# Five opening ticks of a two-stage expert kernel written out one by one, and the second weight matrix loaded behind the first gather

## The chip, the cores and the metric

The kernel runs on one core of a Trainium2 chip. The metric is the device time of one execution in microseconds; times given for the kernel before are 254.93, 255.06 and 255.61 us (median 255.06).

The core's engines run in parallel, each through its own queue in program order, and wait for each other through semaphores: TensorE (PE: matrix products and transposes), VectorE (DVE), ScalarE (ACT), GpSimd (POOL, which also issues the indirect DMAs: gathers and scatters) and SyncE (SP, which issues the plain loads).

## What is computed

Two layers of routed experts on 2048 tokens of width 512:

```python
x = x + _L0_xattn_ref(_layernorm(x, axis=-1), itok_BxS_13_99985, ctx_2048, ctx_2048, ctx_2048)
x = x + _L0_ffn_ref(_layernorm(x, axis=-1), L0_ffn_router_w, L0_ffn_wg, L0_ffn_wu, L0_ffn_wd)
```

The first layer picks one of four experts by the token's id. An expert has one matrix C (512 x 512, the context), used three times:

```python
expert_ids = jnp.minimum(tid // tokens_per_expert, E - 1)
g = jax.nn.silu(jnp.einsum('bsd,fd->bsf', hidden_states, Wg[e]))
u = jnp.einsum('bsd,fd->bsf', hidden_states, Wu[e])
y = jnp.einsum('bsf,df->bsd', g * u, Wd[e])
```

As Wg and Wu are the same matrix, one product a = h C^T serves both. The second layer picks one of eight experts by the largest of eight logits, and its weights are made ternary:

```python
s = 1.0 / jnp.clip(jnp.mean(jnp.abs(w)), EPS, None)
return jnp.clip(jnp.round(w * s), -1.0, 1.0) / s
```

24 weight matrices (1 MB each in 32 bit) have to be loaded, their mean absolute value taken, scaled, rounded and cut. The activations are rounded to eight bits by row.

## The kernel before

Tokens are sorted by expert into blocks of 128 rows: 19 blocks for the first layer (`B1`), 23 for the second (`B2`). The sorting takes the first 10 us. Then a pipeline runs over blocks b. For the first layer, block b passes through:

- POOL `gather(b)` (L465): an indirect DMA brings the block's rows from memory into `x`
- DVE `moments_of`, `aggregate`, `normalise`, `variance`: mean and variance, and `h` = x minus its mean
- PE `transpose_h`; ACT `evict_hT` (L758) writes the transposed rows as the high half `hT_hi`; DVE `hT_rest` (L1083) writes what that leaves out as `hT_lo`
- PE `first_product` (L1585) through `product1` (L1542): three passes of four matmuls of 512 columns, high by high, high by low, low by high halves, with the context's halves `ctx_hi` and `ctx_lo`
- ACT `silu` (L740), DVE `gate` (L1090): p = silu(a) a
- PE `transpose_p`; ACT `evict_pT`, DVE `pT_rest` (L1097); PE `second_product` (L1612): again three passes
- DVE `residual` (L1106) and `negative_mean`: the new row; ACT `square`, DVE `largest` and several small POOL operations (`quantising`): what the second layer's rounding needs
- PE `transpose_x1`, ACT `evict_x1T`, PE `logits`, DVE `top_logits` (L1132), `choice`, `one_hot`, PE `rank` and `count_in`, DVE `row_index`, POOL `place` and `store`: the route of the second layer and a scatter of the rows to scratch memory

`high_halves(e)` (ACT for e = 0 and 1, POOL for 2 and 3) and DVE `low_half(e, part)` (L994) split the context of expert e.

Beside it the weight matrices are made ternary, one a tick: `load_weights(i)` on SP (L364), `sum_abs(i)` on ACT (L680), `sum_mean(i)` on PE (L1566), `mean_of(i)` and `scale_of(i)` on DVE, `scale_part(i)` on both ACT (three quarters) and DVE (one quarter), `cut(i)` on DVE. The matrices 0, 1, 4, 5, ... go through two staging tiles, so `load_weights(4)` waits for both `scale_part(0)`, and `load_weights(5)` for both `scale_part(1)`; 2 and 3 have places of their own. All loads stand in one queue, SP's.

The order on each engine is written by hand. A tick t of the loops (`for t in range(2, TICKS)` on ACT, L843, and DVE, L1392; `for t in range(2, B1)` on PE, L1803) holds first_product(t), second_product(t - 1) and the logits of t - 2; what comes before tick 2 is written out. Before transpose_h(0), PE runs nine matmuls on constants (`warm_up`, L1782), and three behind it. A product on PE waits for its operands before its first pass (`hT_hi` and `ctx_hi` for the first two blocks, `hT_lo` for the others). Of the inputs' 18 blocks in use, block 0 belongs to expert 0, block 1 to expert 1, blocks 2 and 3 to expert 2, and the others to expert 3.

The loads at the start stand on SP in this order:

```python
            load_context(0)
            load_weights(0)
            load_context(1)
            load_weights(1)

            sp.wait_ge(gathering, 2)
            load_context(2)
            load_weights(2)
            load_weights(3)
            load_context(3)
```

`gathering` counts the gathers that POOL has handed out.

## Time and profile before

| | |
|---|---|
| times | 254.93, 255.06, 255.61 us |
| profiled execution | 255.76 us |
| its span | 253.8 us |
| PE busy | 234.7 us (92%) |
| PE weight loads (beside the matmuls) | 172.4 us (68%) |
| DVE busy | 218.2 us (86%) |
| ACT busy | 210.5 us (83%) |
| POOL busy | 164.2 us (65%) |
| loads by SP's queue | 37.91 MB, 42.4% of the DMA engines' time |

The profile is one execution; its times in the rows below are microseconds from the start of its span. A row of the timeline gives start, duration, engine, source line, operation, output and inputs, and in brackets how long the engine idled before it and what ended that. Matmuls overlap, so the distance from one start to the next tells more of their cost than the duration.

### The profile page before, as it was taken

How to read it: one execution, taken by the hardware profiler on the slowest of the kernel's cores; microseconds unless marked ns; L12 is line 12 of the kernel's file. 1: busy time of each engine (PE TensorE's matmuls, PEld its weight loads, DVE VectorE, ACT ScalarE, POOL GpSimd, SP SyncE). 2: the span in 40 equal slices, each digit the busy share in tenths (PEclk: the TensorE clock that was granted, in tenths of full speed). 3: DMA queues.
4: the chain of work that ended last, by engine and by line, in shares of the span. 5: the costliest groups of instructions: out<-in, count | busy, mean ns of one | idle time of the engine just before them, and what ended most of it. 6: DMA issues, size and time to landing. Idle time of an engine off the chain costs nothing.

```text
span 253.8 us, 5722 instructions
## 1 busy us (share of the span) xinstructions
PE 234.7 (92%) x1409; PEld 172.4 (68%) x1419; DVE 218.2 (86%) x675; ACT 210.5 (83%) x324; POOL 164.2 (65%) x325
## 2 busy tenths in 40 slices
PE   2398999999999999999999999999999999999990
PEld 2255778888888888888888888886455555555530
DVE  5879989899889988799888988879999999999871
ACT  2767899799888988898888888787899999999960
POOL 4362665868778777588777664347538786757653
PEclk9999999999999999999999999999999999999996
DMA  5999944935754499784566534541388962211110
GB/s 203 425 359 362 424 180 151 362 131 226 243 210 146 134 354 406 283 324 157 201 249 227 147 127 169 207 146 69 98 237 250 310 251 85 83 41 68 70 37 0
DMA packets 13726, 51.71 MB, mean 204 GB/s; under 512 B 2750, under 2 KB 2750, under 8 KB 10112
## 3 DMA queue, kind: packets, MB, share of 16 engines
q1 hardware_dynamic: 8816, 37.91, 42.4%
q0 software_dynamic: 4880, 13.44, 14.4%
q8 instruction: 14, 0.23, 0.3%
q14 instruction: 16, 0.13, 0.1%
HBM read 40.49 MB, written 13.48 MB: 213 GB/s over the span
## 4 chain that ended last, share of the span: by engine, by line
PE 73%; DVE 10%; DMA 9%; issue 4%; ACT 1%; POOL 1%; SPq 0%; DVEq 0%; ACTq 0%
PE bank L1555 33%; PE bank L1677 19%; PE bank L1539 9%; PE bank L1647 5%; DMA staged<-weight_chunks 4%; PE bank L1669 4%; DMA ternary<-weight_chunks 3%; PE bank L1784 2%; DMA staged<-x_rows 1%; DVE ternary L957 1%; DVE ctx_lo L1000 1%; PE bank L1574 1%; POOL out_rows L643 1%; DVE ternary L1019 1%; DMA token_ids<-token_ids_in 1%
## 5 line engine op out<-in xcount | busy, mean ns | idle before, releaser
L1677 PE MATMUL bank<-ternary,qT 128*128 x179 | 43.6, 380 | 0.5
L694 ACT ACTIVATE ternary<-staged 128x2048 bf16<-128x2048 f32 x20 | 38.0, 1899 | 2.5 <-DMA staged<-weight_chunks 2.5
L700 ACT ACTIVATE ternary<-staged,w_scale 128x1536 int16<-128x1536 f32 x20 | 31.4, 1576 | 2.3 <-DVE w_scale L1014 0.6
L1677 PEld LDWEIGHTS bank<-ternary,qT 128*128 128x128 bf16 x184 | 17.7, 97 | 20.2 <-issue 5.4
L562 POOL DMA_INDIRECT x_rows<-row,store_at x19 | 25.5, 1340 | 6.8 <-POOL store_at L554 5.0
L643 POOL DMA_INDIRECT out_rows<-late_rows,late_token x18 | 19.0, 1057 | 9.4 <-DVE late_rows L1350 8.0
L473 POOL DMA_INDIRECT x<-x_rows,gather x16 | 18.5, 1155 | 10.2 <-DVE gather L969 6.3
L1677 PE MATMUL bank<-ternary,rT 128*128 x87 | 22.6, 380 | 0.4 <-ACT rT L812 0.2
L747 ACT ACTIVATE p<-bank,rstd 128x512 f32<-128x512 f32 x19 | 13.0, 684 | 11.6 <-PE bank L1555 11.5
L1555 PE MATMUL bank<-ctx_hi,pT_hi 128*128 x76 | 22.3, 415 | 0.1
L1555 PE MATMUL bank<-ctx_hi,hT_hi 128*128 x76 | 22.3, 414 | 0.0
L1094 DVE SCALAR_TENSOR_TENSOR p<-bank,rstd,p 128x512 f32<-128x512 f32 x19 | 14.2, 749 | 9.3 <-ACT p L747 9.3
L1647 PEld LDWEIGHTS bank<-router,x1T 128*128 128x128 f32 x152 | 19.7, 191 | 1.9 <-ACT x1T L756 0.6
L1555 PE MATMUL bank<-ctx_lo,hT_hi 128*128 x76 | 20.4, 391 | 0.3 <-DVE ctx_lo L1000 0.3
L1555 PE MATMUL bank<-ctx_lo,pT_hi 128*128 x76 | 20.5, 392 | 0.0
L1555 PE MATMUL bank<-ctx_hi,pT_lo 128*128 x76 | 20.5, 392 | 0.0
L1555 PE MATMUL bank<-ctx_hi,hT_lo 128*128 x76 | 20.3, 389 | 0.0
L517 POOL TENSOR_TENSOR row<-ln,half_powers 128x2 f32<-128x2 f32 x19 | 14.5, 763 | 8.8 <-DVE squares L1129 8.7
L1647 PE MATMUL bank<-router,x1T 128*128 128x8 f32 x152 | 18.2, 247 | 0.1
L489 POOL TENSOR_TENSOR rstd<-var_eps,half_powers 128x1 f32<-128x1 f32 x19 | 13.7, 719 | 5.3 <-DVE var_eps L1070 4.8
L1305 DVE TENSOR_TENSOR prod<-bank,relu 128x512 f32<-128x512 f32 x23 | 15.8, 686 | 1.5 <-ACT relu L790 0.6
L1555 PEld LDWEIGHTS bank<-ctx_lo,hT_hi 128*128 128x128 f32 x76 | 14.2, 188 | 3.6 <-issue 0.7
(237 smaller groups left out, 658.6 us busy)
## 6 DMA issues: line engine op xcount, KB each, us to landing
staged<-weight_chunks SPq DMA_DIRECT2D x20, 1024.0 KB, 5.5
late_rows<-x_rows SPq DMA_DIRECT2D x18, 260.0 KB, 3.7
ternary<-ctx_chunks SPq DMA_DIRECT2D x4, 1024.0 KB, 8.3
ternary<-weight_chunks SPq DMA_DIRECT2D x4, 1024.0 KB, 9.8
x_rows<-filler SPq DMA_DIRECT2D x1, 2080.0 KB, 12.9
staged<-x_rows SPq DMA_DIRECT2D x5, 260.0 KB, 2.7
x_rows<-row,store_at POOLq DMA_INDIRECT x19, 6.0
out_rows<-late_rows,late_token POOLq DMA_INDIRECT x18
```

Of the source, the lines that this page charges most:

```text
L473: pool.indirect_dma_start(x[b % RING], None, x_in, bass.IndirectOffsetOnAxis(ap=gather1[:, b:b + 1], axis=0), bounds_check=last_token, oob ...
L517: pool.tensor_tensor(r[:, RSTD:INV + 1], s[:, 2:4], half_powers[:, :], ALU.pow).then_inc(norm2, 1)
L562: pool.indirect_dma_start(x1_rows, bass.IndirectOffsetOnAxis(ap=store_at[b % ROWS][:, :], axis=0), row[b % ROWS][:, :], None, bounds_check ...
L643: pool.indirect_dma_start(out, bass.IndirectOffsetOnAxis(ap=token, axis=0), cols_of([b], 0, D), None, bounds_check=last_token, oob_is_err= ...
L694: nc.scalar.activation(ternary[:, m * K * D:(m + 1) * K * D], staged_of(i), ACT.Abs, accum_out=abs_sum[:, 2 * i:2 * i + 1]).then_inc(abs_r ...
L700: nc.scalar.activation(ternary[:, m * K * D + DVE_COLS:(m + 1) * K * D].bitcast(I16), staged_of(i)[:, DVE_COLS:], ACT.Copy, scale=w_scale[ ...
L1094: dve.scalar_tensor_tensor(p[:, :], a_ps[b % 2][:, :], rstd1[b % 2][:, :], p[:, :], ALU.mult, ALU.mult).then_inc(p_ready, 1)
L1305: dve.tensor_tensor(prod[b % 2][:, :], u_ps[b % 2][:, :], relu2[:, :], ALU.mult)\
L1539: last = pe.transpose(ps[:, k * P:(k + 1) * P], src[:, k * P:(k + 1) * P], ident[:, :])
L1555: last = pe.matmul(ps[:, :], left[:, k * P:(k + 1) * P], right[:, bass.ds(e * (K * D) + k * D, D)], start=(n == 0 and k == 0), stop=(n == ...
L1647: last = pe.matmul(logits_ps[:, 0:E2], x1T[:, k * P:(k + 1) * P], router[:, k * E2:(k + 1) * E2], start=(k == 0), stop=(k == K - 1))
L1677: last = pe.matmul(ps[:, :], left[:, k * P:(k + 1) * P], ternary[:, bass.ds(e * (3 * K * D) + (kind * K + k) * D, D)], start=(k == 0), sto ...
```

## The change

On SP, the second weight matrix is issued once the first gather is handed out; context 2 and weights 2 follow once the second gather is, weights 3 once context 2 has landed, and context 3 once weights 2 has. On ACT, DVE and PE, ticks 2 to 4 are written out operation by operation in a new order, and the loops begin at tick 5 (`OPENING`). Seven matmuls stand ahead of transpose_h(0) in place of nine. `product1` can run other work of PE ahead of its second or third pass (`ahead`), and the products of blocks 1 to 3 wait for less at their start: the first product for `hT_hi` and the high halves of the context, the second product of block 0 for `pT_hi`. The work done is the same.

```diff
-WARM_UP = (9, 3)
+WARM_UP = (7, 3)
+OPENING = 5
...
             load_context(1)
+            sp.wait_ge(gathering, 1)
             load_weights(1)
-
             sp.wait_ge(gathering, 2)
+
             load_context(2)
             load_weights(2)
+            sp.wait_ge(ctx_in_sem[2], 16)
             load_weights(3)
+            sp.wait_ge(staged_early_in[0], 16)
             load_context(3)
```

ScalarE:

```diff
             high_halves(1)
-            sum_abs(1)
             evict_hT(0)
             scale_part(0)
+            sum_abs(1)
+            evict_hT(1)
+            silu(0)
+            sum_abs(2)
+            evict_pT(0)
             scale_part(1)
-            silu(0)
-            evict_hT(1)
-            evict_pT(0)
-            sum_abs(2)
             silu(1)
             evict_hT(2)
+            sum_abs(3)
             scale_part(2)
-            sum_abs(3)
-            for t in range(2, TICKS):
+            evict_pT(1)
+            evict_x1T(0)
+            square(0)
+            silu(2)
+            sum_abs(4)
+            evict_hT(3)
+            evict_pT(2)
+            scale_part(3)
+            scale_part(4)
+            sum_abs(5)
+            silu(3)
+            square(1)
+            evict_hT(4)
+            evict_x1T(1)
+            scale_part(5)
+            evict_pT(3)
+            sum_abs(6)
...
+            for t in range(OPENING, TICKS):
```

VectorE, the added order of the first ticks (the removed one is in the listing above):

```diff
+            low_half(0, 0)
             mean_of(0)
-            scale_of(0)
-            low_half(0, 0)
             moments_of(0)
             aggregate(0)
             normalise(0)
-            variance(0)
             low_half(0, 1)
-            mean_of(1)
-            scale_of(1)
-            hT_rest(0)
-            low_half(1, 0)
+            scale_of(0)
             moments_of(1)
             aggregate(1)
             normalise(1)
+            hT_rest(0)
+            variance(0)
             variance(1)
-            scale_part(0)
-            gate(0)
-            hT_rest(1)
+            low_half(1, 0)
             low_half(1, 1)
...
             moments_of(2)
             aggregate(2)
             normalise(2)
+            gate(0)
+            hT_rest(1)
+            mean_of(1)
+            scale_of(1)
+            low_half(2, 0)
             variance(2)
+            scale_part(0)
+            pT_rest(0)
+            low_half(2, 1)
             mean_of(2)
             scale_of(2)
+            gate(1)
             moments_of(3)
             aggregate(3)
+            residual(0)
+            negative_mean(0)
+            hT_rest(2)
+            normalise(3)
             variance(3)
+            scale_part(1)
+            moments_of(4)
+            mean_of(3)
+            scale_of(3)
+            aggregate(4)
+            pT_rest(1)
+            gate(2)
+            low_half(3, 0)
+            low_half(3, 1)
+            mean_of(4)
+            scale_part(2)
+            scale_of(4)
+            residual(1)
+            negative_mean(1)
+            hT_rest(3)
+            scale_part(3)
+            scale_part(4)
+            top_logits(0)
+            choice(0)
+            one_hot(0)
+            pT_rest(2)
+            normalise(4)
+            largest(0)
+            moments_of(5)
+            variance(4)
+            mean_of(5)
+            gate(3)
+            scale_of(5)
+            row_index(0)
+            aggregate(5)
+            variance(5)
+            cut(4)
+            residual(2)
+            negative_mean(2)
+            scale_part(5)
+            hT_rest(4)
+            largest(1)
+            top_logits(1)
+            choice(1)
+            one_hot(1)
+            normalise(5)
+            pT_rest(3)
+            largest(2)
+            gate(4)
...
+            cut(5)
```

TensorE, the waits and the new order:

```diff
-            def first_product(b):
+            def first_product(b, ahead={}):
...
-                if b < 2:
+                if b < E1:
                     pe.wait_ge(hT_hi_ready, b + 1)
-                    pe.wait_ge(ctx_hi_ready, b + 1)
+                    pe.wait_ge(*((ctx_hi_ready, b + 1) if b < 2 else (pool_hi_ready, b - 1)))
                     pe.wait_ge(centred, 1)
                 else:
                     pe.wait_ge(hT_lo_ready, b + 1)
...
             transpose_h(0)
-            sum_mean(1)
             warm_up(WARM_UP[1])
             first_product(0)
             load_expert(1)
             transpose_h(1)
-            transpose_p(0)
-            first_product(1)
+            sum_mean(1)
+
+            def in_first1():
+                transpose_p(0)
+            first_product(1, {2: in_first1})
             load_expert(2)
             transpose_h(2)
-            sum_mean(2)
-            second_product(0)
-            for t in range(2, B1):
+
+            def in_second0():
+                sum_mean(2)
+            second_product(0, {1: in_second0})
+
+            def in_first2():
+                transpose_p(1)
+                transpose_x1(0)
+                sum_mean(3)
+            first_product(2, {2: in_first2})
+            load_expert(3)
+            transpose_h(3)
+            second_product(1)
+            transpose_p(2)
+            sum_mean(4)
+
+            def in_first3():
+                logits(0)
+            first_product(3, {2: in_first3})
+            load_expert(4)
+            transpose_x1(1)
+
+            def in_second2():
+                rank(0)
+                sum_mean(5)
+                transpose_h(4)
+            second_product(2, {2: in_second2})
+            transpose_p(3)
+
+            def in_first4():
+                logits(1)
+            first_product(4, {2: in_first4})
+            load_expert(5)
+            count_in(0)
+            transpose_x1(2)
+            transpose_h(5)
+            rank(1)
+            sum_mean(6)
+            second_product(3)
+            logits(2)
+            count_in(1)
+            for t in range(OPENING, B1):
```

## Rows read from the trace of the kernel before

**Rows 1.** Page, the chain that ended last: shares of the span by engine.

```profile
PE 73%; DVE 10%; DMA 9%; issue 4%; ACT 1%; POOL 1%; SPq 0%; DVEq 0%; ACTq 0%
```

**Rows 2.** Stretches: start:end, length, busy PE, PEld, DVE, ACT, POOL, PEclk, DMA share, GB/s.

```profile
12.69:16.51 3.82, 3.82 (x10) 1.38 (x11) 2.93 (x7) 2.81 (x3) 2.10 (x4) 1.00 0.98 360
16.51:30.57 14.06, 12.62 (x61) 9.27 (x59) 13.18 (x25) 10.09 (x11) 6.93 (x6) 1.00 1.01 386
...
55.60:63.59 7.99, 7.99 (x51) 6.82 (x51) 7.45 (x25) 7.63 (x12) 7.00 (x12) 1.00 0.54 203
```

**Rows 3.** Timeline (start, us, engine, line), TensorE: opening to the first second_product.

```profile
12.69 4.02 PE L1784 MATMUL bank<-iota 128*128 128x512 f16 x9 [0.29 <-issue]
...
16.51 1.06 PE L1539 MATMUL bank<-ident,h 128*128 128x128 f32 x4
...
17.56 0.81 PE L1784 MATMUL bank<-iota 128*128 128x512 f16 x3
...
18.34 1.17 PE L1555 MATMUL bank<-ctx_hi,hT_hi 128*128 x4
...
27.73 1.17 PE L1555 MATMUL bank<-ctx_hi,pT_hi 128*128 x4
```

**Rows 4.** Timeline, TensorE: tick 3 from first_product to tick 5.

```profile
39.62 1.17 PE L1555 MATMUL bank<-ctx_hi,hT_hi 128*128 x4
...
42.48 0.63 PE L1539 MATMUL bank<-ident,row 128*128 128x128 f32 x4
...
43.68 1.19 PE L1555 MATMUL bank<-ctx_hi,pT_hi 128*128 x4
...
46.54 0.95 PE L1647 MATMUL bank<-router,x1T 128*128 128x8 f32 x8
...
47.37 0.64 PE L1539 MATMUL bank<-ident,p 128*128 128x128 f32 x4
...
47.76 1.17 PE L1555 MATMUL bank<-ctx_hi,hT_hi 128*128 x4
...
55.60 0.64 PE L1539 MATMUL bank<-ident,p 128*128 128x128 f32 x4
```

**Rows 5.** Timeline, VectorE: moments and h of block 0.

```profile
14.80 0.69 DVE L1058 BATCH_NORM_STATS2 stats<-x 128x6 f32<-128x512 f32 x1 [0.81 <-DMA x<-x_rows,gather]
...
15.74 0.49 DVE L1080 TENSOR_SCALAR h<-x,moments 128x512 f32<-128x512 f32 x1
```

**Rows 6.** Timeline, VectorE, ticks 3 and 4.

```profile
40.12 0.68 DVE L1114 SCALAR_TENSOR_TENSOR row<-bank,x 128x512 f32<-128x512 f32 x1
...
40.73 0.17 DVE L1136 MAX8 best<-bank 128x8 f32<-128x8 f32 x1
...
41.41 0.48 DVE L1080 TENSOR_SCALAR h<-ternary,moments 128x512 f32<-128x512 f32 x1
...
44.21 0.75 DVE L1094 SCALAR_TENSOR_TENSOR p<-bank,rstd,p 128x512 f32<-128x512 f32 x1
...
45.74 0.68 DVE L1087 TENSOR_TENSOR hT_lo<-bank,hT_hi 128x512 fp32r<-128x512 f32 x1
...
47.36 0.69 DVE L1025 TENSOR_SCALAR ternary<-ternary 128x2048 bf16<-128x2048 int16 x1
```

**Rows 7.** Timeline, ScalarE: an evict_hT, sum_abs(2), a silu.

```profile
17.60 0.60 ACT L764 ACTIVATE hT_hi<-bank 128x512 fp32r<-128x512 f32 x1 [1.52 <-PE bank L1539]
...
24.79 1.91 ACT L694 ACTIVATE ternary<-ternary 128x2048 bf16<-128x2048 f32 x1 [0.60 <-DMA ternary<-weight_chunks]
...
43.46 0.68 ACT L747 ACTIVATE p<-bank,rstd 128x512 f32<-128x512 f32 x1
```

**Rows 8.** DMA issues in 11.7:12.5 us (gather 1); last figure: us, issue to landing.

```profile
x<-x_rows,gather POOLq DMA_INDIRECT x1, 3.6
```

**Rows 9.** DMA issues in 13:13.3 us (gather 2).

```profile
x<-x_rows,gather POOLq DMA_INDIRECT x1, 9.7
```

**Rows 10.** DMA issues in 40:41 us (a load alone in its queue).

```profile
staged<-weight_chunks SPq DMA_DIRECT2D x1, 1024.0 KB, 4.8
```

72 lines of the change are left out of this document (36 added, 36 removed).

## The prediction

> **What bounds the kernel now.** I read the chain that ended last first [rows 1]: 73% of it is TensorE (PE), so time is to be had only where PE waits. Then the stretches [rows 2]: from 55.60 us a tick of 7.99 us has 7.99 us of PE work, and it stays so for the rest of the first product stage. The opening, 16.51 to 30.57, has 12.62 busy of 14.06 us, at a DMA share of 1.01 and with VectorE (DVE) busy for 13.18. So the change can win only what PE idles before 55.60, which is where tick 5 begins, with the same work done in both kernels: from there both run the same loop. My whole sum is one number: when transpose_p(4) starts in the new kernel, against 55.60 [rows 4].
>
> Short names: F, S are first_product and second_product, Th, Tp, Tx the three transposes, each with its block. PE work, from the distance of one start to the next [rows 4]: F 2.83 (39.62 to about 42.45), S 2.86, logits 0.81, Tp 0.39; Th and Tx about 0.45 (an estimate between Tp and the 0.6 that one lasts); sum_mean, rank and count_in together 0.2 a tick. A product's last result is 0.16 later than the next start. Handing on between engines costs 0.03 to 0.13. DVE, start to start [rows 5, 6]: gather landed to h 1.43 (14.80 to 15.74 + 0.49), low_half 1.13 (an estimate: about 1.8 times the 0.61 of residual, for twice the columns), gate 0.67, hT_rest 0.61 with its result at 0.68, residual 0.8 with its accumulator and negative_mean, top_logits to one_hot 0.68, scale_part 0.4, cut 0.61. ScalarE (ACT) [rows 7]: sum_abs 1.9, evict_hT 0.60, silu 0.68; scale_part lies between, about 1.5.
>
> **The change part by part.** *Start.* Nine warm-ups take 12.69 to 16.51, 0.425 each [rows 3]; seven end at 15.66. h(0) is wanted by then. Gather 0 is issued at about 10.3, and its data were waited for until 14.80 [rows 5]; gather 1 took 3.6 us [rows 8]. With weights 1 out of the way I take 3.6 for gather 0 too, so 13.9, and h(0) at 15.35: transpose_h(0) starts at 15.66, a gain of 0.85. Between the ends 3.6 and 4.5 I take the lower, because the queue is then empty behind context 1. Part of the gain goes back at once: the nine warm-ups run at 512 columns in 0.425 us, the level of 1.2 GHz, the later three in 0.81 together [rows 3], which is 2.4 GHz (the clock column says 1.00 for both, so it can't be used here). PE rose between 16.51 and 17.56, with the engine busy since 12.69. If it rises at the same moment, the three late warm-ups start 1.05 us earlier and run partly at the low level: F0 starts at 17.48 to 17.8; I take 17.65 against 18.34, as the middle.
>
> *F0 to S0.* F0 ends at 20.5; Th(1); ACT evicts it by 21.8, after sum_abs(1). That sum now stands behind scale_part(0), which ends at 18.7; weights 1, issued at about 11.75 and not at 3, lands at 16.6 to 18 (4.8 us alone in its queue [rows 10], plus gathers), so its cover is 0.7 us and the cost is nothing. F1 starts at 21.9, with 0.8 us of idle PE. ctx_lo(1) is now ready at 21.1, since both its halves stand before moments_of(2), so nothing waits inside F1; Tp(0) goes in before its third pass, and Th(2) ends PE's work at 25.7. S0 needs evict_pT(0), which stands behind sum_abs(2) on ACT: everything on ACT waits for weights 2 there. Before, weights 2 was there at 24.79 [rows 7]. Now it shares the queue with weights 1 and context 2 alone (weights 3 is issued once context 2 is in, context 3 once weights 2 is): three loads of 1.05 MB and about 0.55 MB of gathers are 3.7 MB, from 13.5 on (issue, and the part of the 4.8 us that isn't transfer) at the 360 to 386 GB/s of [rows 2] 9.6 to 10.3 us, so 23.1 to 23.8, or 22.3 if the gathers are through early; I take 22.9. Then 1.9 + 0.6 + handing on: S0 starts at 25.7, against 27.73 [rows 3]. That is the change's whole gain, 2.0 us. Each us that weights 2 lands after 23.0 costs 1.0; at 24.7, as before, 1.65.
>
> *S0 to F3.* Work: 2.86 + 0.14, then 2.83 + 0.39 + 0.45 + 0.14 (F2 with Tp(1), Tx(0) and a mean inside), 0.45, 2.86, 0.39 + 0.14 = 10.65, plus 0.15 of wait for pT_rest(1): F3 at 36.5. F3 to S2: 2.83 + logits(0) 0.81 + Tx(1) 0.45 = 4.1, but pT_rest(2) follows top_logits, choice and one_hot of block 0, which need logits(0): 0.15 more. S2 at 40.85. Weights 3 and 4 have 2 us and more of cover here: weights 4 is issued at 25.7, late by 4 us since scale_part(0) on DVE moved back, and wanted at 33.5. On the POOL queue gather 3 now stands behind the inverse deviation of block 0, 2 us later, wanted at 28.2. largest(0) comes much later too, so quantising(0) on POOL ends only just before residual(2) needs it; what that could cost is in the upper end.
>
> *S2 to F4, where the gain is lost.* F4 waits for hT_rest(4) (block 4 takes the branch of b >= E1). On DVE that stands behind residual(2), negative_mean(2) and scale_part(5), and residual(2) needs the end of S2. Chain from S2's start: two passes, a rank and sum_mean(5) 2.25; mean_of(5) was waiting for that; then gate(3) 0.67, cut(4) 0.61 and five small ones about 0.6 (three dependent ones take 0.68 [rows 6]): 4.15. S2 itself is ready at 3.6, so DVE is the later. Then 0.8 + 0.4 + 0.68 + 0.05: F4 starts 6.1 after S2, at 46.95. PE has 2.86 + 0.17 + 0.45 + 0.39 = 3.87 of work in it: 2.2 us idle. Had DVE come in time, it would still be 0.16 + 0.8 + 0.4 + 0.68 + 0.05 - 0.39 = 1.7. Before, F4 started at once behind Tp(3), 0.39 after 47.37 [rows 4].
>
> *F4 to tick 5.* 2.83 + 0.81 + 0.45 + 0.45 + 0.2 + 2.86 + 0.81 = 8.4, nothing waits: the chain from logits(1) over one_hot, normalise(5) and pT_rest(3) takes 1.8, PE's way to S3 2.0, so that is covered by only 0.2. Tick 5 at 55.4.
>
> The sum: 25.7 + 10.8 + 4.35 + 6.1 + 8.45 = 55.4 against 55.60, 0.2 us less. The profiled execution took 255.76 us (span 253.8), the median of the three runs is 255.06, 0.7 less; so 255.56 for such an execution, and **254.9 us** for the median.
>
> **The rivals.** A measurement of this kernel can tell about 0.3%, 0.77 us, from no change.
>
> *A, the forecast:* 2.0 us won by S0, given back ahead of F4. 254.9, own range 254.3 to 255.8. Chance 0.45.
>
> *B, faster:* DVE reaches residual(2) before S2 ends (idle 1.7 and not 2.2), the two small waits of 0.15 are not there, and F0 starts at 17.48: 0.95 less, 254.0. For it speaks that hand-offs are summed on the slow side; against it that the stall's 1.7 is fixed by the order of the program. Chance 0.28.
>
> *C, slower: gather 2 isn't there when it is wanted.* moments_of(2) now comes at 20.85, ahead of gate(0) and no longer behind it; gate(0) stands behind it, and Tp(0) and all of PE behind gate(0). Gather 2 took 9.7 us from 13.1 [rows 9], so 22.8. With up to 0.75 of slack, it costs one for one from 21.6 on: 1.2 at 22.8, so 256.1; slower than before by over 0.3% from 22.5 on. For it: the DMA share is about 1 in both, and issue is no earlier. Against: gathers 1 [rows 8] and 0 took 3.6 and 4.5 while at most two loads stood ahead, 9.7 was with four issued behind it. The Trainium skill, "DMA: Bandwidth & Descriptors" (Arbitration), says that an engine takes turns between its queues packet by packet; by that rule two loads in the queue or four make no difference to a gather, and the time would be the 256.1 of this case. The rows lean against the rule (3.6 and 9.7 at the same share), though not by an experiment. Chance 0.17.
>
> *D, slower: the clock.* PE idles 2.2 us before F4. The opening of before has 1.44 us of idle PE in all (14.06 less 12.62 [rows 2]), and no single gap of 2.2. At the low level F4's twelve matmuls take 5.1 us (0.425 each [rows 3]) and not 2.83: 257.2. The Trainium skill, "TensorE: Matmul & The Clock Gate" (The HAM clock gate), has the array fall back after idling; the trace can't show whether this gap is enough. Chance 0.05.
>
> *E, it doesn't do what it says:* gather 0 lands at 14.78 as before, h(0) at 16.25, 0.6 lost: 255.5. Chance 0.05.
>
> **How the numbers follow.** Faster is B, 0.28; within 0.3% is A and E, 0.50; slower is C and D, 0.22. Range: down to B with 0.4 for the hand-offs, 253.6; up past C to the case that weights 2 lands at 24.7 (254.9 + 1.65 = 256.55), 256.7. D is left out.
>
> **What would show it.** transpose_h(0) at 15.7, F0 at 17.6, F1 at 21.9, S0 at 25.7 or a wait of ACT for weights 2 ahead of it; F3 about 3 us before 39.62 (2.3 of it real, since logits(0) is inside it now); a 2 us hole of PE ahead of the product of block 4, released by DVE's hT_lo; transpose_p(4) at 55.4, then ticks of 7.99. The forecast is wrong if that hole is not there, if the opening loses to a landing (moments_of(2) idle for a gather, sum_abs(2) for weights), or if the twelve matmuls of block 4 last 5 us.

## The result, and the profile after

The changed kernel takes 261.45 us (median; 261.4 to 262.84), against 255.34 us (254.93 to 255.88) for the kernel before on the same chip: a ratio of 1.025, 95% interval 1.021 to 1.029. It is slower by 2.5%, where 254.9 us was forecast. The profiled execution took 261.4 us, its span 259.4. It can be set beside the 255.76 us and 253.8 of the kernel before: 5.6 more.

The forecast was one walk to the start of transpose_p(4), tick 5. The TensorE rows of the timeline after (start, us, engine, line, operation; in brackets the idle time before it and what ended that) go through the same points:

```profile
15.64 1.06 PE L1613 MATMUL bank<-ident,h 128*128 128x128 f32 x4
...
17.47 1.51 PE L1632 MATMUL bank<-ctx_hi,hT_hi 128*128 x4
...
21.34 1.19 PE L1632 MATMUL bank<-ctx_hi,hT_lo 128*128 x4 [1.46 <-DVE hT_lo L1116]
...
23.74 1.19 PE L1632 MATMUL bank<-ctx_hi,hT_hi 128*128 x4 [0.65 <-ACT hT_hi L772]
24.77 1.09 PE L1632 MATMUL bank<-ctx_lo,hT_hi 128*128 x4
28.08 0.97 PE L1613 MATMUL bank<-ident,p 128*128 128x128 f32 x4 [2.21 <-DVE p L1123]
28.70 2.06 PE L1632 MATMUL bank<-ctx_hi,hT_lo 128*128 x4
30.55 1.06 PE L1613 MATMUL bank<-ident,h 128*128 128x128 f32 x4
31.26 1.36 PE L1632 MATMUL bank<-ctx_hi,pT_hi 128*128 x4
...
42.11 1.17 PE L1632 MATMUL bank<-ctx_hi,hT_hi 128*128 x4
...
46.47 1.20 PE L1632 MATMUL bank<-ctx_hi,pT_hi 128*128 x4
...
52.72 1.19 PE L1632 MATMUL bank<-ctx_hi,hT_hi 128*128 x4 [2.03 <-DVE hT_lo L1116]
...
61.36 0.64 PE L1613 MATMUL bank<-ident,p 128*128 128x128 f32 x4
```

| point or stretch | forecast | after | before [rows 3, 4] |
|---|---|---|---|
| transpose_h(0) | 15.66 | 15.64 | 16.51 |
| F0 | 17.65 | 17.47 | 18.34 |
| F1 | 21.9 | 23.74 | |
| S0 | 25.7 | 31.26 | 27.73 |
| S0 to F3 | 10.8 | 10.85 | |
| F3 to S2 | 4.35 | 4.36 | |
| S2 to F4, with the hole | 6.1 | 6.25 | |
| F4 to tick 5 | 8.45 | 8.64 | |
| tick 5 | 55.4 | 61.36 | 55.60 |

Tick 5 is 5.76 us later than before, and that is the whole 5.6: from there the tick takes 7.99 us again, with PE busy throughout, as in [rows 2]. S0 came 5.56 us later than walked, although F0 began 0.18 early: the miss lies between these two points. The four stretches behind S0 came within 0.2 us each, 0.4 together. Three things happened ahead of S0.

*Gather 1 was late.* VectorE stood 2.58 us for it (first row below is gather 0, which came as forecast), and hT_rest(0), put behind normalise(1) by the new order, stood behind that. F0's third pass waited 1.46 us for it, and F1 started at 23.74.

```profile
14.04 0.69 DVE L1087 BATCH_NORM_STATS2 stats<-x 128x6 f32<-128x512 f32 x1 [0.83 <-DMA x<-x_rows,gather]
...
19.25 0.69 DVE L1087 BATCH_NORM_STATS2 stats<-x 128x6 f32<-128x512 f32 x1 [2.58 <-DMA x<-x_rows,gather]
```

The DMA issues of 11.7:11.9 us after (first fence: the last figure is us from issue to landing) give gather 1 7.4 us, where [rows 8] had 3.6. The shares of the two queues in 13.8:14.2 us of the kernel before (second fence) and in 14.6:15.2 of the one after (third) tell why. In the kernel before, weights 1 had just been through and context 2 had not begun, so GpSimd's queue (software) had the engines to itself. In the kernel after, weights 1 was flowing on SyncE's queue (hardware), and between 14.0 and 15.5 us no packet of a gather moved, though two gathers were handed out at 11.79 and 13.10. From 16.5 to 19.5 us, beside context 2, they had 27.7% of the engines' time.

```profile
x<-x_rows,gather POOLq DMA_INDIRECT x1, 7.4
```

```profile
q0 software_dynamic: 42, 0.14, 97.7%
```

```profile
q1 hardware_dynamic: 32, 0.26, 104.2%
```

*normalise(2) took 2.83 us in place of 0.49.* In the new order it stands ahead of gate(0), on which transpose_p(0) and all of PE wait. It ended at 27.36, which is 0.29 us after GpSimd's cast of context 2 ended (25.17 + 1.90 = 27.07). VectorE and GpSimd after:

```profile
24.53 2.83 DVE L1109 TENSOR_SCALAR h<-x,moments 128x512 f32<-128x512 f32 x1
27.29 0.74 DVE L1123 SCALAR_TENSOR_TENSOR p<-bank,rstd,p 128x512 f32<-128x512 f32 x1
```

```profile
25.17 1.90 POOL L489 CAST ctx_hi<-ternary 128x2048 fp32r<-128x2048 f32 x1
```

*TensorE's clock fell in the hole.* PE stood 2.21 us ahead of transpose_p(0). The windows after (us; busy us and count for PE, PE's weight loads, VectorE, ScalarE, GpSimd; granted clock, DMA share, GB/s) show a granted clock of 0.57 and 0.58 behind it, so for most of these 4 us the lower level, 1.2 GHz in place of 2.4:

```profile
26.00:28.00 2.00, 0.00 (x0) 0.00 (x0) 2.00 (x3) 0.07 (x1) 1.82 (x2) 1.00 0.93 360
28.00:30.00 2.00, 1.92 (x7) 1.70 (x8) 1.97 (x7) 0.91 (x2) 0.31 (x1) 0.57 0.88 326
30.00:32.00 2.00, 2.00 (x8) 1.63 (x8) 2.00 (x5) 2.00 (x3) 0.67 (x1) 0.58 0.71 158
```

F1's third pass was 1.85 us ahead of the next start, transpose_h(2) 0.71. Without the fall the same two take 1.05 and 0.35 (e4 below: 27.72, 28.77, 29.12). That is 1.16 us by S0, and 0.18 more in S0's first pass.

Together: 1.84 (F1 late) + 2.21 (hole) + 1.16 (clock) + 0.23 (from transpose_p(0) to F1's third pass, 0.62 and not 0.39) = 5.44 of the 5.56. The 0.23 is a wait that the walk had left out: the third pass needs hT_lo(1), and hT_rest(1) stands behind gate(0) on VectorE, where it took 27.95 to 28.63; the pass began at 28.70.

### The profile page after: what moved, and what is told of

It reads as the page before. It is cut to its first block, busy times and chain, and to the rows that moved or that the text cites. A ratio compares the mean times of both kernels' runs of the same rounds, so it can differ in the third digit from the quotient of the medians.

```text
span 259.4 us, 5720 instructions
## 1 busy us (share of the span) xinstructions
PE 235.9 (91%) x1407; PEld 173.8 (67%) x1417; DVE 219.5 (85%) x675; ACT 210.0 (81%) x324; POOL 162.8 (63%) x325
## 4 chain that ended last, share of the span: by engine, by line
PE 80%; DVE 10%; DMA 4%; issue 3%; POOL 1%; SPq 0%; DVEq 0%
PE bank L1632 40%; PE bank L1759 19%; PE bank L1613 10%; PE bank L1729 6%; PE bank L1751 4%; DMA x<-x_rows,gather 3%; DVE h L1109 1%; DMA staged<-x_rows 1%; PE bank L1651 1%; DVE ternary L986 1%; DVE ctx_lo L1029 1%; POOL out_rows L651 1%; DMA token_ids<-token_ids_in 1%; DVE late_rows L1379 1%; DVE p L1123 1%
## 5 line engine op out<-in xcount | busy, mean ns | idle before, releaser
L570 POOL DMA_INDIRECT x_rows<-row,store_at x19 | 24.5, 1292 | 6.8 <-POOL store_at L562 5.9
L1123 DVE SCALAR_TENSOR_TENSOR p<-bank,rstd,p 128x512 f32<-128x512 f32 x19 | 14.2, 749 | 10.5 <-ACT p L755 10.3
L1632 PE MATMUL bank<-ctx_hi,hT_lo 128*128 x76 | 21.7, 410 | 1.5 <-DVE hT_lo L1116 1.5
L497 POOL TENSOR_TENSOR rstd<-var_eps,half_powers 128x1 f32<-128x1 f32 x19 | 14.1, 741 | 12.4 <-DVE var_eps L1099 11.9
L1632 PEld LDWEIGHTS bank<-ctx_hi,hT_lo 128*128 128x128 f32 x76 | 14.4, 195 | 4.6 <-DVE hT_lo L1116 1.9
## 6 DMA issues: line engine op xcount, KB each, us to landing
x_rows<-filler SPq DMA_DIRECT2D x1, 2080.0 KB, 12.6
```

The lines of the kernel that those rows point to most:

```text
L570: pool.indirect_dma_start(x1_rows, bass.IndirectOffsetOnAxis(ap=store_at[b % ROWS][:, :], axis=0), row[b % ROWS][:, :], None, bounds_check ...
L1123: dve.scalar_tensor_tensor(p[:, :], a_ps[b % 2][:, :], rstd1[b % 2][:, :], p[:, :], ALU.mult, ALU.mult).then_inc(p_ready, 1)
L1632: last = pe.matmul(ps[:, :], left[:, k * P:(k + 1) * P], right[:, bass.ds(e * (K * D) + k * D, D)], start=(n == 0 and k == 0), stop=(n == ...
```

## The experiments

Every ratio is against the kernel before, run on the same chip, with its 95% interval in brackets. 0.003 is about what can be told from 1. F, S, Th, Tp are the names of the prediction. A time in brackets after a start is the idle time before it.

### Loads and order apart: e1_loads_only, e2_order_only

e1 is the kernel before with the new loads; e2 is the changed kernel with the old ones. The edit of e2 (that of e1 is the same lines the other way round):

```diff
             load_context(1)
-
-            sp.wait_ge(gathering, 1)
             load_weights(1)
+
             sp.wait_ge(gathering, 2)
-
             load_context(2)
             load_weights(2)
-            sp.wait_ge(ctx_in_sem[2], 16)
             load_weights(3)
-            sp.wait_ge(staged_early_in[0], 16)
             load_context(3)
```

> The kernel before, with the new order of loads alone. Theory (gather 1 was slowed by weights 1, which now starts beside it): gather 1 takes about 7 us and not 3.6, but costs nothing here, because VectorE comes to moments_of(1) only at about 20; weights 1 lands at 16.6 and sum_abs(1) stands ahead of evict_hT(0) on ScalarE, so first_product(0) starts at 19.3 and not 18.34, and the kernel takes 1.1 us more, 256.4. Rival (the loads have nothing to do with it): gather 1 takes 3.6 to 4.5 us and the time stays at 255.3. Second rival (the loads are all of the loss): 261.

> The changed kernel with the loads in the order of before. Theory: gather 1 takes 3.6 to 4.5 us again and the 2.6 us idle of VectorE before moments_of(1) is gone; gather 2 takes 9.7 us again and lands at 22.8, weights 2 at 24.7, so second_product(0) starts at about 27.4, the 2.2 us hole ahead of the product of block 4 stays: 256.9. Rival (the new order loses by itself, whatever the loads do): 261.

Measured: e1 1.010 [1.006, 1.013], e2 1.017 [1.011, 1.023]. Each half costs by itself, and both expectations were too good (1.1 us over 255.3, or 1.004, and 256.9, or 1.006). The rival of e2, that the new order loses by itself (261, or 1.022), lies inside its interval. In e1, weights 1 comes later, and in the old order ScalarE's sum_abs(1) stands ahead of evict_hT(0), and sum_mean(1) ahead of PE's three warm-ups. PE stood 2.12 us, and F0 began at the lower clock. TensorE of e1:

```profile
18.96 0.38 PE L1578 MATMUL bank<-abs_sum,ones 128*128 128x1 f32 x2 [2.12 <-ACT ternary L698]
...
20.01 2.27 PE L1559 MATMUL bank<-ctx_hi,hT_hi 128*128 x4
```

In e2, with weights 1 issued at once, gather 1 took 4.2 us, VectorE did not wait for it, and F1 started at 21.97, where 21.9 had been walked. The 1.46 us wait of F0 is gone. The collision with the cast (normalise(2) 2.45 us) and the fall of the clock stayed. VectorE, then TensorE of e2:

```profile
22.97 2.45 DVE L1105 TENSOR_SCALAR h<-x,moments 128x512 f32<-128x512 f32 x1
```

```profile
26.14 0.66 PE L1609 MATMUL bank<-ident,p 128*128 128x128 f32 x4 [2.06 <-DVE p L1119]
26.74 2.07 PE L1628 MATMUL bank<-ctx_hi,hT_lo 128*128 x4
```

So the late gather comes from the loads, the collision from the order. e2 also speaks against my reading that a gather is slow by the number of loads issued behind it: gather 2 took 8.9 us in e2 with all loads issued and 8.2 in the changed kernel with two.

### One cause at a time in the changed kernel: e3_cast_held, e4_filled, e5_weights1_last, e6_rest4_early

e3 holds GpSimd's cast of context 2 until normalise(2) is through:

```diff
                 pool.wait_ge(ctx_in_sem[e], 16)
+                if e == 2:
+                    pool.wait_ge(h_ready, 3)
                 pool.tensor_copy(
```

> The changed kernel, where GpSimd's cast of context 2 (high_halves(2)) waits for h(2). Theory (VectorE's normalise(2) lasted 2.83 us because it was shut out until GpSimd's cast had ended, and PE's clock fell in the hole that this made): normalise(2) lasts 0.5 to 1 us, transpose_p(0) starts at 25.8 and not 28.08, the matmuls behind it run at the high level: 3.7 us less, 257.7. Rival (the 2.83 us have another cause, as the inverse deviation or the gather's descriptors): normalise(2) stays near 2.8 us and the time at 261.4. If only the lock is right and not the clock: 259.1.

Measured: 1.027 [1.022, 1.032], no gain at all, though what was meant to happen did: normalise(2) 0.49 us, Tp(0) at 25.94, S0 at 27.93, 3.3 us earlier than after. VectorE and GpSimd of e3:

```profile
24.74 0.49 DVE L1111 TENSOR_SCALAR h<-x,moments 128x512 f32<-128x512 f32 x1
...
36.54 0.69 DVE L1089 BATCH_NORM_STATS2 stats<-ternary 128x6 f32<-128x512 f32 x1 [1.64 <-DMA ternary<-x_rows,gather]
```

```profile
25.61 1.89 POOL L491 CAST ctx_hi<-ternary 128x2048 fp32r<-128x2048 f32 x1
27.68 2.02 POOL L481 DMA_INDIRECT ternary<-x_rows,gather  x1 [0.18 <-issue]
```

The gain went to the next thing that was late. The new order has moments_of(4) ahead of pT_rest(1). Gather 4, which stands behind the cast on GpSimd, was issued at 27.68 (27.25 after), and its data ended VectorE's wait at 36.54, 8.9 us later (5.1 us of transfer after). S1 stood 2.45 us for pT_rest(1), and F4 2.03 us as before. The profiled execution of e3 took 265.84 us, 2.65 over its median, with a mean granted clock of 0.972; behind the 2.45 us its rows show the lower level too (S1's first pass 1.87 us from start to start), and again inside F4, so in this execution part of what was won went there.

e4 gives PE eight matmuls on constants ahead of Tp(0), so that the hole is there for everyone but the clock:

```diff
             def in_first1():
+                warm_up(8)
                 transpose_p(0)
```

> The changed kernel with eight matmuls on constants put into the hole of PE ahead of transpose_p(0), 1.7 of its 2.2 us. Theory (PE's clock fell because it idled there): the granted clock stays 1.00 between 28 and 32 us, transpose_p(0) starts at 28.1 as before, and the 1.4 us that the low level took are saved: 260.0. Rival (the clock fell for another reason, or its fall costs nothing, since other engines are late there too): 261.4 or more.

Measured: 1.020 [1.012, 1.027], 259.97 us, about as expected (260.0, a ratio of 1.018). normalise(2) was still 2.83 us and ended 0.28 after the cast, PE stood only 0.48 us, and the clock stayed:

```profile
27.12 0.66 PE L1613 MATMUL bank<-ident,p 128*128 128x128 f32 x4 [0.48 <-DVE p L1123]
27.72 1.21 PE L1632 MATMUL bank<-ctx_hi,hT_lo 128*128 x4
```

The pass that took 2.06 us after takes 1.21, and from Tp(0) to S0 e4 takes 2.00 us, the changed kernel 3.18. The ratios differ by 0.6%, 1.4 us, but their intervals overlap ([1.012, 1.027] and [1.021, 1.029]), and gather 1 took 6.5 us here, so that F1 started 0.95 us earlier. So what the filling is worth in the whole time isn't shown; what the clock costs is read from the rows. One of e4's four executions took 262.82 us with a mean granted clock of 0.978 (the others 0.994 to 0.996), so filling this one hole doesn't keep the clock up every time.

e5 issues weights 1 behind gathering 2, so that nothing flows beside gather 1; e6 puts hT_rest(4) ahead of cut(4) and residual(2):

```diff
-            sp.wait_ge(gathering, 1)
-            load_weights(1)
             sp.wait_ge(gathering, 2)
+            load_weights(1)
 
             load_context(2)
```

```diff
+            hT_rest(4)
             cut(4)
             residual(2)
             negative_mean(2)
             scale_part(5)
-            hT_rest(4)
```

> The changed kernel with weights 1 issued behind the second gather and not behind the first. Theory (a gather is slow when a large load flows beside it, and how many stand in the queue matters little): gather 1 takes 4 to 5 us and not 7.4, the 2.6 us of VectorE before moments_of(1) and the 1.5 us inside first_product(0) go, second_product(0) starts 1.5 us or more earlier than 31.3 at the same hole ahead of transpose_p(0): 259.5. Rival (gather 1 is slow because gather 0 goes before it, or by its own rows): gather 1 stays at 7 us, the time at 261.4.

> The changed kernel with hT_rest(4) on VectorE moved ahead of cut(4), residual(2), negative_mean(2) and scale_part(5). Theory (first_product(4) waits only for that position): its wait shrinks from 2.0 us to 0.3 or less and the time falls by 1.7 to 2.0: 259.5. Rival (what is late there is ScalarE's evict_hT(4), or the loss comes back a step later because residual(2) is now late): 261.4, with a new wait of second_product(3).

Measured: e5 1.011 [1.008, 1.014], e6 1.011 [1.007, 1.014]; 259.5 us had been expected of both, which against the 255.34 us of then is 1.016, so both are better by about 0.5%. In e5 gather 1 took 4.0 us, F1 started at 21.60, S0 at 27.12; normalise(2) was 2.37. (S1 then stood 1.69 us for pT_lo: VectorE's scale_part(1) took 2.06 us beside the second cast, that of context 3.) The DMA queues of e5 in 14.0:14.6 us, where after only the hardware queue moved data:

```profile
q0 software_dynamic: 37, 0.14, 96.9%
q1 hardware_dynamic: 2, 0.02, 10.1%
```

Here the clock fell elsewhere, in the hole ahead of F4, for which the forecast had 2.2 us:

```profile
50.38 1.96 PE L1631 MATMUL bank<-ctx_hi,hT_hi 128*128 x4 [2.04 <-DVE hT_lo L1115]
52.13 1.91 PE L1631 MATMUL bank<-ctx_lo,hT_hi 128*128 x4
```

That is one execution, of 260.81 us, 1.65 over the median. Five of the other seven have a mean granted clock of 0.993 to 0.996, where it has 0.987, so these had less of a fall or none.

In e6 that hole is gone (F4 at 49.91, 0.16 us idle before it), which was worth about 2 us, but F1 ran at the lower clock (its first pass 1.87 us from start to start), behind a wait of 1.90 us inside F0.

### The order with the old loads and the cast held: e10_old_loads_held

e2 and e3 together.

> The changed kernel with the loads of before and with the cast of context 2 held until h(2) is there, so without both causes. Theory (beside these two and what the clock adds, the walk of the prediction holds): first_product(1) at 22.0, transpose_p(0) at 24.2 with no fall of the clock there, second_product(0) at 27.4 because sum_abs(2) waits for weights 2 until 24.7, then 10.8 + 4.4 + 6.2 + 8.5 us to tick 5 at 57.3: 256.8; up to 3 us more where gather 4, handed out behind the cast, is late, or the clock falls in the hole before first_product(4). Rival (a further cause is missing): second_product(0) later than 28.5.

Measured: 259.41 us, 1.016 [1.008, 1.023]; but its four times are 257.42, 258.01, 260.81 and 260.96, and the profiled one is the 257.42. In it gather 1 took 3.8 us, normalise(2) 0.49, S0 started at 26.60, and only the hole ahead of F4 was left (48.73, 2.03 idle) with no fall of the clock. 256.8 was expected; 257.42 has that mechanism. Two of the others are 3.4 us higher. Their mean granted clock was 0.979 and 0.978, that of the other two 0.995, so the clock did fall in them. No profile shows where: the fall that a profile shows alone (f5, below) cost 1.62 us, so it was longer here or came twice.

### The cast held, and moments_of(4) later: f1_held_4_later

e3 failed by moments_of(4) standing ahead of pT_rest(1). f1 is e3 with

```diff
-            moments_of(4)
             mean_of(3)
             scale_of(3)
-            aggregate(4)
             pT_rest(1)
             gate(2)
+            moments_of(4)
+            aggregate(4)
```

> The changed kernel with the cast of context 2 held until h(2), and moments_of(4) with aggregate(4) behind gate(2), so that a late gather 4 holds nothing up. Theory (the run with the cast held alone lost its 3.3 us again because gather 4 came late and PE's clock fell twice more): normalise(2) lasts 0.5 us, second_product(0) starts at 28, second_product(1) within 0.5 us of PE being free, and where the clock doesn't fall ahead of first_product(4) the kernel takes 3 us less than the changed one, ratio to before 1.012; where it falls there, 1.02. Rival (holding the cast costs as much as it saves): 1.025.

Measured: 1.019 [1.015, 1.023], at the upper end of what was expected (1.012 to 1.02), and 0.8% below e3: the wait for gather 4 was real (S1 started without a wait). Gather 1's wait (2.20 us ahead of F0's third pass) and the hole ahead of F4 (2.04) are still there, and its rows show the lower level behind both (F1's first pass 1.87 us from start to start, F4's second 1.68). The profiled execution took 264.36 us, 3.2 over the median, so these falls are not those of a typical one.

### All of it mended: e9_mended, f2_mended_weights1_last

e9 has the cast held, moments_of(4) later, hT_rest(4) early, and weights 1 issued at once, with the later loads still two at a time. f2 is the same with weights 1 issued behind gathering 2, as in e5.

> The changed kernel mended: weights 1 loaded at once as before, the later loads still two at a time, the cast of context 2 held until h(2), moments_of(4) behind gate(2), hT_rest(4) ahead of cut(4). Theory: no idle time of PE above 1.5 us, so the clock never falls; weights 2 lands at 23 to 24, second_product(0) starts at 26 to 26.8, tick 5 begins 27.9 - 2.0 us later, at 52.0 to 52.7, and the kernel takes 252 to 253, less than both. Rival (moved work is late elsewhere): 255 to 256.

> The changed kernel with weights 1 behind both gathers, the cast held, moments_of(4) behind gate(2), hT_rest(4) ahead of cut(4). Theory: transpose_h(0) at 15.7, gathers 0 and 1 take 4 us each, no hole of PE above 1 us, granted clock 1.00 throughout; weights 2 still lands at 24.2, so second_product(0) starts at 26.7 as in the other mended kernel, and the early start is lost ahead of it: ratio to before 0.998 to 1.000. Rival (the 0.6 us of the start carry through): 0.997.

Measured: e9 255.97 us, 1.000 [0.998, 1.002]; f2 256.19 us, 1.0015 [0.9995, 1.0035]. With these four places mended together the 2.5% are gone; what each takes of it by itself is not in these two runs. f2 lies a little above what was expected of it (0.998 to 1.000). The 252 to 253 us that I expected of e9 are not there; its rival (255 to 256) was right. In its profile S0 starts at 26.72, 1.0 earlier than in [rows 3], and tick 5 at 55.74, against 55.60. ScalarE stood for weights 2, 1.3 us later than walked (22.9), and the second cast made normalise(3) 1.25 us:

```profile
24.18 1.91 ACT L702 ACTIVATE ternary<-ternary 128x2048 bf16<-128x2048 f32 x1 [1.81 <-DMA ternary<-weight_chunks]
```

### Can the order win? f3_pT_first, f6_both_held

f3 is f2 with evict_pT(0) ahead of sum_abs(2) and evict_hT(2) and silu(1) ahead of scale_part(1) on ScalarE, and sum_mean(2) behind S0 on PE (not in the cut below), so that S0 no longer waits for weights 2:

```diff
             silu(0)
-            sum_abs(2)
             evict_pT(0)
-            scale_part(1)
-            silu(1)
+            sum_abs(2)
             evict_hT(2)
+            silu(1)
+            scale_part(1)
             sum_abs(3)
```

> The same with evict_pT(0) ahead of sum_abs(2) on ScalarE, evict_hT(2) and silu(1) ahead of scale_part(1), and sum_mean(2) behind second_product(0). Theory (what holds second_product(0) is the landing of weights 2, through its place in ScalarE's queue): it starts at 25.8 and not 26.7, first_product(2) at 28.9 and not 29.8, and the kernel takes 0.9 us less than before: ratio 0.9965. Rival (mean_of(2) on VectorE is now late and holds gate(1)): 1.000 or more.

Measured: 256.13 us, 1.001 [0.9995, 1.0025]. S0 started at 26.10, 1.6 us earlier than before, and that was lost at the second cast (context 3), which met scale_part(1). VectorE and GpSimd of f3:

```profile
32.83 2.05 DVE L1049 TENSOR_SCALAR ternary<-staged,w_scale 128x512 int16<-128x512 f32 x1
```

```profile
32.55 2.05 POOL L490 CAST ctx_hi<-ternary 128x2048 fp32r<-128x2048 f32 x1 [4.12 <-DMA ternary<-ctx_chunks]
```

It ended at 34.88, 0.28 after the cast, and S1 stood 1.65 us for pT_rest(1). f6 holds that cast too, until scale_part(1) is through, and has evict_pT(1) ahead of scale_part(2):

```diff
                 if e == 2:
                     pool.wait_ge(h_ready, 3)
+                if e == 3:
+                    pool.wait_ge(dve_part, 2)
```

> The mended kernel in which evict_pT(0) and evict_hT(2) stand ahead, and in which GpSimd's second cast (context 3) is also held, until VectorE's scale_part(1) is through, with evict_pT(1) ahead of scale_part(2) on ScalarE. In that kernel without the two last edits scale_part(1) took 2.05 us beside the cast, and second_product(1) waited 1.65 us for pT_lo, at 35.80. If the cast was the whole of that wait, scale_part(1) takes 0.48, second_product(1) starts at 34.1 to 34.7, tick 5 at 54.9 to 55.5, and the ratio is 0.995 to 0.999: what the new order is worth with both locks away. Rival: the next thing is late (weights 4, evict_x1T(0), the later cast), second_product(1) at 35 or later or a new wait before tick 5, and the ratio is 0.999 to 1.003.

Measured: 256.63 us, 1.005 [1.003, 1.007]: the rival, and more than it said. scale_part(1) took 0.48 us, S0 started at 25.59 and S1 at 33.74 (35.80 in f3; 34.1 to 34.7 expected). TensorE of f6 then shows new waits one after the other:

```profile
33.74 1.19 PE L1635 MATMUL bank<-ctx_hi,pT_hi 128*128 x4
...
37.40 0.38 PE L1654 MATMUL bank<-abs_sum,ones 128*128 128x1 f32 x2 [0.21 <-ACT ternary L705]
37.97 1.19 PE L1635 MATMUL bank<-ctx_hi,hT_hi 128*128 x4 [0.19 <-ACT hT_hi L775]
...
43.02 1.20 PE L1635 MATMUL bank<-ctx_hi,pT_hi 128*128 x4 [0.44 <-DVE pT_lo L1135]
...
47.40 1.18 PE L1635 MATMUL bank<-ctx_hi,hT_hi 128*128 x4 [0.16 <-DVE hT_lo L1119]
```

Tick 5 is at 56.04. From S0 to tick 5 f6 takes 30.45 us, the kernel before 27.87 [rows 3, 4]. The windows between the two points (columns as above), f6 first, then the kernel before:

```profile
25.59:56.04 30.45, 29.14 (x162) 23.51 (x160) 26.33 (x78) 28.75 (x39) 18.05 (x27) 1.00 0.75 277
```

```profile
27.73:55.60 27.87, 27.53 (x159) 23.12 (x158) 25.32 (x74) 25.40 (x35) 17.80 (x33) 1.00 0.64 242
```

PE idles 1.31 us against 0.34, and is busy for 1.6 us more with nearly the same matmuls. Of the 1.6, sum_mean(2), now behind S0, is 0.14. An operation put between two passes makes the next pass cost about 0.1 more: F4's three passes take 1.02 + 0.92 + 1.02 = 2.96 us in the changed kernel (52.72, 53.74; 55.46 behind logits(1)), and 2.83 unbroken in f4, below; there are four such breaks in the stretch, some 0.4 us. The rest, an estimate, is the 0.16 us by which a product's last result trails, which counts as busy wherever PE then waits. So what S0 wins is paid back in small waits and breaks, and no kernel of this study beats the one before.

### The two disputed costs by themselves: f4_collision, f5_hole_left

Up to here the cast and the flowing loads always came together. f4 is the kernel before with one wait more, so that its cast of context 2 meets its normalise(2):

```diff
                 pool.wait_ge(ctx_in_sem[e], 16)
+                if e == 2:
+                    pool.wait_ge(stats_ready, 3)
                 pool.tensor_copy(
```

> The kernel before, in which GpSimd's cast of context 2 also waits for the statistics of gathering 2 (nothing else is changed), so that it starts beside normalise(2) and not 1.8 us ahead of it. If the cast shuts VectorE out by itself, as I now read the 2.83 us normalise(2) of the changed kernel, then normalise(2) takes about 2.0 us in place of 0.59 and ends some 0.3 us behind the cast, T_h of tick 2 starts at about 28.6 us in place of 27.09, the second product some 1.3 us later, and the ratio is 1.004 to 1.007 (1.010 to 1.015 if TensorE's granted clock falls in the hole). Rival, that normalise(2) was long for another reason (the loads that flow, the reads of the gathered rows): it keeps 0.5 to 0.6 us here, and the ratio is 0.998 to 1.003.

Measured: 257.43 us, 1.004 [1.003, 1.006], as expected. VectorE, GpSimd and TensorE of f4:

```profile
26.59 2.09 DVE L1082 TENSOR_SCALAR h<-x,moments 128x512 f32<-128x512 f32 x1
```

```profile
26.51 1.89 POOL L483 CAST ctx_hi<-ternary 128x2048 fp32r<-128x2048 f32 x1 [4.10 <-DVE stats L1060]
```

```profile
28.74 0.66 PE L1541 MATMUL bank<-ident,h 128*128 128x128 f32 x4 [1.80 <-DVE h L1082]
```

normalise(2) went from 0.59 to 2.09 us and ended at 28.68, 0.28 after the cast. The loads and the gathers up to gather 3 are untouched, so the cast by itself does it. The hole of 1.80 us in PE brought no fall of the clock here.

f5 is f2 with hT_rest(4) back where the change had it, which leaves the hole ahead of F4 as the only fault.

> The mended kernel with weights 1 last, in which hT_rest(4) is back where the change put it, behind residual(2), first_product(3) and cut(4). This measures the hole ahead of first_product(4) alone, with every other fault of the opening taken away. If the hole costs what it measures, first_product(4) waits about 2.0 us again, tick 5 is 2.0 us later (57.8 in place of 55.8), and the ratio is 1.008 to 1.011; if the granted clock falls in the hole as it did in two of the earlier runs, 1.5 to 3 us more, and the ratio is 1.014 to 1.022. Rival, that the hole is filled by work that is late anyway: the ratio stays within 0.999 and 1.004.

Measured: 259.64 us (258.25 to 262.08), 1.014 [1.005, 1.022], so 1.2% over f2. TensorE of f5:

```profile
50.20 2.01 PE L1633 MATMUL bank<-ctx_hi,hT_hi 128*128 x4 [2.03 <-DVE hT_lo L1117]
52.01 1.87 PE L1633 MATMUL bank<-ctx_lo,hT_hi 128*128 x4
```

From S2 to F4 it took 6.28 us, f2 4.38: 1.90 for the hole. From F4 to tick 5 10.22 us against 8.60: 1.62 for the clock that fell in it. By S2 it was 1.07 us behind f2 already, with a wait of 0.97 for the sum of weights 4 on the way. (The profiled execution took 260.64 us, 1.0 over the median.) The other three fit this: 258.25 and 258.64 us at a mean granted clock of 0.993 and 0.994, 2.1 to 2.5 over f2's median, the hole alone; and 262.08 at 0.978.

## Why the prediction was wrong

*What bounds the kernel, and the sum by tick 5.* Right: everything that changed lies before tick 5, and the difference there (5.76) is the difference of the executions (5.6).

*Start.* Right. Gather 0 took 3.8 us (3.6 taken), Th(0) 15.64, F0 17.47. The early start had a price that the walk left out, in F0 itself, whose first pass ran partly at the lower level: 1.34 us from start to start, where rows at the higher one give 1.02. It cost nothing here, since F0 waited behind it anyway.

*F0 to S0* is the step that failed. The walk had PE busy from F1 (21.9) to S0 (25.7) with no wait in it; PE came to F1 1.84 us late and then stood 2.21 us. Three things were mispriced or left out:

- The price of gather 1. The walk has no term for it: it reaches F1 as if gather 1 took the 3.6 us of [rows 8] again. That row was fast for a reason that the change takes away: in it the gather fell into the gap between weights 1 and context 2, and the change puts weights 1 exactly beside it. Measured 7.4, which delayed hT_rest(0) behind it by enough to move F1 by 1.84. e2, e5 and e9 give 4.2, 4.0 and 3.9 with no load flowing from about 13.5 to 14.7 us. I had the question right only for gather 2 (rival C), one gather too late.
- The cover of VectorE's operations beside GpSimd's cast. The walk took 0.49 us for normalise(2) [rows 6] and never asked what GpSimd does at that moment. It costs 1.5 to 2.4 us in every run where the two meet in full (after, e2, e4 to e6, f4). The kernel before holds a hint, a normalise(2) of 0.59 beside the end of the cast, too small to see as a stall because the old order has normalise(2) late, and the meeting cost it only 0.1. f4 shows the cause alone.
- The clock. Rival D had it at 2.3 us for a whole product at the lower level (1.34 measured after, 1.62 in f5, since it rose again before twelve such matmuls were through) and named the wrong hole: I had only the 2.2 us ahead of F4 in mind, as a single case of 0.05, and behind that one the clock stayed up in the profiled execution. There was a second hole, and the profiles of e1, e2, e3, e5, e6, f1 and f5 show falls as well, in one place or the other.

*S0 to F3, F3 to S2.* Right: 10.85 and 4.36 for 10.8 and 4.35. That was partly luck, since all of PE was 5.6 us late and every load had that much cover. With PE on time (e3, f5, f6) moments_of(4) waited 1.64 us for gather 4, or PE for weights 4 (0.97), so "2 us and more of cover" was too good. (The walk's own terms for F3 to S2 add up to 4.25 and not to the 4.35 that went into its sum.)

*S2 to F4.* Right: 6.25 for 6.1, and the hole of 2.03 released by hT_lo, as named. e6 and f5 show that it costs those 2 us (1.90).

*F4 to tick 5.* 8.64 for 8.45 (the terms as written add up to 8.41). 0.13 of the difference is the product with logits(1) put inside it, which I took at 2.83 all the same.

*Rivals.* C (256.1) reached its number by gather 2 standing in VectorE's way; gather 2 took 8.2 us and VectorE didn't wait for it, being late itself; where it was on time, in e2 and e5, it waited 0.29 and 0.38 us. What C rested on was right: the rows that I set against the rule, 3.6 and 9.7 us at the same DMA share, didn't differ by the number of loads in the queue but by whether one was flowing. The Trainium skill, "DMA: Bandwidth & Descriptors" (Arbitration), has each DMA engine take turns, packet by packet, between the queues that have work for it. By that rule the number of loads behind in a queue doesn't matter, and the runs agree (8.9 us with all issued, 8.2 with two). An even exchange they don't show: in 14.0 to 15.2 us after, the hardware queue alone had 92 to 104% of the engines' time and no gather packet moved. The gathers had been handed out: in e5, issued at the same moments, they had 96.9% in 14.0 to 14.6 us.

The range, 253.6 to 256.7, was made of slips of one term at a time. The outcome was three at once, and they weren't all independent: the meeting with the cast makes the hole, and behind the hole the clock fell, which in the profile of e4, where it is filled, it didn't. The late gather came beside them; e2 and e5 have the meeting without it.

## What to carry to other kernels

A duration taken from the trace of before holds only beside what ran beside it: before using a gather's 3.6 us, look at which other queue moved data in just those microseconds, and before moving a VectorE operation that reads and writes the on-chip memory, at what GpSimd does at its new place. When work is put in a new order by hand, walk VectorE and GpSimd against each other, not PE alone, and price every hole of about 2 us twice, once for itself and once for the clock. Where PE is busy for 12.6 of 14.1 us, a new order can win 1 us and lose 6; mending its faults here brought back the time of before, and no more.

## What the runs showed of the hardware that I had not expected

- **GpSimd's cast and VectorE's scaling exclude each other.** VectorE's tensor_scalar from memory to memory (128x512, normally 0.48 us) ended 0.27 to 0.30 us after the end of GpSimd's 128x2048 cast wherever it began beside a running cast, save in its last 0.03 us (before, e1, e5, e9, f3, f4), and also in five runs where it began 0.16 to 0.64 us ahead of the cast (after, e2, e4 to e6; 24.53 and 25.17 after). It went the other way where GpSimd had been idle for over 2 us ahead of the cast and VectorE had begun 0.03 to 0.2 us before it: the scaling kept its 0.48 us, and the cast took 2.03 to 2.20 us in place of 1.90 (the first row of the second fence below). Two other operations of VectorE kept their 0.68 beside the cast, as GpSimd and VectorE of the kernel before show (pT_rest reads TensorE's bank, batch_norm_stats the memory):

```profile
24.67 2.09 POOL L481 CAST ctx_hi<-ternary 128x2048 fp32r<-128x2048 f32 x1 [2.40 <-DVE ctx_lo L1000]
```

```profile
24.52 0.48 DVE L1019 TENSOR_SCALAR ternary<-staged,w_scale 128x512 int16<-128x512 f32 x1
24.91 0.68 DVE L1103 TENSOR_TENSOR pT_lo<-bank,pT_hi 128x512 fp32r<-128x512 f32 x1
25.52 0.68 DVE L1058 BATCH_NORM_STATS2 stats<-x 128x6 f32<-128x512 f32 x1
...
26.45 0.59 DVE L1080 TENSOR_SCALAR h<-x,moments 128x512 f32<-128x512 f32 x1
```

The Trainium skill, "SBUF — State Buffer" (SBUF: two separate sides), describes a port pair that GpSimd shares with some of VectorE's operations as an exclusive lock, held for the whole instruction, the loser blocked until the end. The trace agrees with that, f4 above all (0.59 to 2.09). It also says that whichever starts first gets the pair. The rows with an idle GpSimd agree; by the starts in the rows after, VectorE was first and still lost. In all five such runs GpSimd went from a gather and the inverse deviation straight into the cast. Who held the pair at 24.53 the trace doesn't tell: in e3, with the same two operations before but the cast held, normalise(2) began at the same point of them and took 0.49.
- **A gather can get nothing for over a microsecond beside a flowing load.** Gather 1 took 3.6 to 4.5 us where no load flows from about 13.5 to 14.7 us, and 6.3 to 7.6 where weights 1 does; gather 2 took 7.4 to 9.7 beside the loads that follow. The kernel before shows the same with gather 0, which took 4.5 us there and 3.8 after: in 12.0 to 13.0 us weights 1 had 98.5% of the engines' time and no gather packet moved, and after, with no load flowing, the gather had 80.3%. Beside context 2 (16.5 to 19.5 us after) the gathers had 27.7%, so it isn't so beside every load, and these runs don't show why.
- **The granted clock falls after holes of about 2 us, in some and not in others.** It fell behind 2.45 (e3), 2.21 (after), 2.20 (f1), 2.12 (e1), 2.06 (e2), 2.03 to 2.04 (e3, e5, f1 and f5, at F4) and 1.90 us (e6); it stayed behind 2.03 to 2.04 (after, e2, e4 and e10, at F4), 1.95 (e3) and 1.80 us (f4). The same kernel does either: the executions of e5, e10 and f5 have mean granted clocks from 0.978 to 0.996. Rows wholly at the lower level give 1.71 to 1.87 us from start to start for a pass of four matmuls, in place of 0.91 to 1.02. What decides between the two, I can't say from these runs; where the hole was filled with matmuls on constants (the profile of e4) it did not fall.
